# Multiplying the first three patches of an early-fusion block side by side, one piece of weights at a time

## The reference, cut to what matters

```python
xc = jnp.concatenate([x] + [_shift2d(x, HALF * s[2], HALF * s[0]) for s in shifts], axis=1)
patches = ...                      # [32, 36, 3840]
xn = (patches - mu) * jax.lax.rsqrt(var + LN_EPS) * ln_gamma + ln_beta
h = jnp.einsum('bnp,dp->bnd', xn, W) + b
h = jnp.concatenate([h, txt], axis=1)          # 36 patches and 128 text tokens
h = h + attention(layernorm(h))                # a decaying linear memory, 8 heads
h = h + experts(layernorm(h))                  # 2 of 8 gated experts per token
```

## Time and profile before

| | us |
|---|---|
| median of 3 runs | 548.85 (548.56 to 549.72) |
| span of the profiled execution | 547.2 |
| median less span | 1.65 |
| PE busy | 484.7 (89%) |
| DVE busy | 375.3 (69%) |
| ACT busy | 304.8 (56%) |
| mean granted TensorE clock | 0.962 |

### The profile page before, as it was taken

One profiled execution on the slowest core, in us unless ns is written; L12 is line 12 of the kernel. 1 busy time (PEld: TensorE's weight loads), 2 busy tenths in 40 slices (PEclk: granted clock), 3 DMA queues, 4 the chain that ended last, 5 costly groups with the idle time before them and its releaser, 6 DMA issues.

```text
span 547.2 us, 12568 instructions
## 1 busy us (share of the span) xinstructions
PE 484.7 (89%) x3157; PEld 461.4 (84%) x3158; DVE 375.3 (69%) x1293; ACT 304.8 (56%) x773; POOL 192.3 (35%) x272
## 2 busy tenths in 40 slices
PE   2999998998798987789999999999999999999900
PEld 2999997887576876789999999999999999999800
DVE  4969996459789879848566566565565565565597
ACT  5485967449578876435444444444444444444473
POOL 1000000006577777733333333333433433433330
PEclk9999999999799989799999999999999999999965
DMA  8988214711433342542222222222222222235897
GB/s 322 415 331 350 63 53 130 283 38 51 120 94 110 101 126 76 139 117 73 71 76 76 68 79 73 68 82 70 68 83 69 69 83 68 68 84 145 273 353 223
DMA packets 62463, 71.67 MB, mean 131 GB/s; under 512 B 19057, under 2 KB 56626, under 8 KB 61410
## 3 DMA queue, kind: packets, MB, share of 16 engines
q1 hardware_dynamic: 49920, 51.43, 30.6%
q0 software_dynamic: 8208, 16.95, 8.7%
q10 hardware_dynamic: 4306, 2.95, 1.8%
HBM read 49.43 MB, written 21.86 MB: 130 GB/s over the span
## 4 chain that ended last, share of the span: by engine, by line
PE 71%; DVE 15%; DMA 6%; ACT 4%; issue 2%; ACTq 1%; SPq 0%; POOL 0%; DVEq 0%; POOLq 0%
PE bank L838 8%; PE pair L838 6%; PE bank L1088 5%; PE bank L1084 5%; PE bank L1087 5%; PE bank L1086 5%; PE bank L1085 5%; PE bank L1095 5%; PE pair L1104 4%; PE bank L1104 4%; PE pair L1073 3%; PE pair L983 3%; ACT yall L749 2%; PE pair L987 2%; PE pair L1106 2%
## 5 line engine op out<-in xcount | busy, mean ns | idle before, releaser
L782 POOL DMA_INDIRECT disp<-xf,posu x82 | 85.0, 1037 | 151.0 <-ACT xf L654 123.8
L1575 DVE TENSOR_TENSOR hh<-sg,bank 128x384 f32<-128x384 f32 x89 | 49.3, 554 | 99.5 <-ACT sg L730 99.5
L812 POOL DMA_INDIRECT ydram<-ysb,dnow x89 | 88.5, 994 | 69.4 <-DMA ydram<-ysb,dnow 35.1
L730 ACT ACTIVATE sg<-bank 128x384 f32<-128x384 f32 x89 | 43.7, 492 | 116.8 <-PE bank L1088 116.8
L1084 PE MATMUL bank<-wa,xh 128*128 x178 | 67.5, 379 | 0.0
L1088 PE MATMUL bank<-wa,xl 128*128 x178 | 60.4, 339 | 0.0
L1087 PE MATMUL bank<-wa,xh 128*128 x178 | 59.9, 337 | 0.0
L1085 PE MATMUL bank<-wa,xh 128*128 x178 | 59.7, 336 | 0.0
L1086 PE MATMUL bank<-wa,xl 128*128 x178 | 59.7, 335 | 0.0
L809 POOL COPY dnow<-dest 128x1 uint32 (+1 forms) x89 | 16.9, 190 | 114.2 <-DVE ysb L1585 104.8
L838 PE MATMUL bank<-wcT,imgT 128*128 128x193 f32 x240 | 41.7, 335 | 10.6 <-DMA imgT<-in_pixels 10.6
(11 more groups left out here) (262 smaller groups left out, 1171.2 us busy)
## 6 DMA issues: line engine op xcount, KB each, us to landing
xs<-disp SPq DMA_DIRECT2D x89, 96.0 KB, 2.0
band<-in_bands SPq DMA_DIRECT2D x4, 1536.0 KB, 12.1
yall<-ydram SPq DMA_DIRECT2D x7, 768.0 KB, 7.8
imgT<-in_pixels SPq DMA_DIRECT2D x4, 768.0 KB, 12.5
imgT<-in_pixels SPq DMA_DIRECT2D x2, 1536.0 KB, 16.0
hres<-in_text SPq DMA_DIRECT2D x1, 3072.0 KB, 25.5
wa<-in_gate_up_w SPq DMA_DIRECT2D x8, 384.0 KB, 8.5
ring<-in_gate_up_w SPq DMA_DIRECT2D x32, 96.0 KB
```

Of the source, the lines that this page charges most:

```text
L782: pool.indirect_dma_start(disp, bass.IndirectOffsetOnAxis(ap=posu[c % XBUF][:, 2 * j + k:2 * j + k + 1], axis=0), xfd[c % XBUF][:, j, :], None
L812: pool.indirect_dma_start(ydram, bass.IndirectOffsetOnAxis(ap=dnow[b][:], axis=0), ysb[r][:], None).then_inc(s_ys[b], 16)
```

## The change

Pixels and weights come in pairs: behind piece g of the weights, row block g of the pixels with all four column blocks. PE multiplies patches 0, 1 and 2 by piece g before it goes on to piece g+1, each patch in its own bank; the three groups of sums are open at the same time. The two bands follow all four pairs; before, they stood ahead of the last pixels that patch 2 reads.

```diff
-            weights_in(0)
-            weights_in(1)
-            pixels_in(0, slice(0, 2), slice(0, 2))
-            weights_in(2)
-            pixels_in(1, slice(2, 4), slice(0, 2))
-            weights_in(3)
-            pixels_in(2, slice(0, 4), 2)
+            for g in range(4):
+                weights_in(g)
+                pixels_in(g, slice(g, g + 1), slice(0, 4))
             for i in range(2):
                 sp.dma_start(band[i][:], bands[:, i]).then_inc(s_band[i], 16)
-            pixels_in(3, slice(0, 4), 3)
             pixels_in(4, slice(4, 6), slice(0, 4))
...
             def patch(p):
-                i, j = p // 3, p % 3
-                if p:
-                    pe.wait_ge(s_img[1 + j if i == 0 else 3 + i], 16)
+                if p % 3 == 0:
+                    pe.wait_ge(s_img[3 + p // 3], 16)
                 if p >= 4:
                     pe.wait_ge(s_patout, p - 3)
...
-            for p in range(3):
-                patch(p)
+            for dr in range(4):
+                pe.wait_ge(s_wprep, dr + 1)
+                pe.wait_ge(s_img[dr], 16)
+                for p in range(3):
+                    ins = pixel_row(p, dr)
+                    if dr == 3:
+                        ins.then_inc(s_pat, 1)
```

More of the change, by code:

```diff
@@ L826, in patch, with pixel_row @@
             def patch(p):
-                i, j = p // 3, p % 3
-                if p:
-                    pe.wait_ge(s_img[1 + j if i == 0 else 3 + i], 16)
+                if p % 3 == 0:
+                    pe.wait_ge(s_img[3 + p // 3], 16)
                 if p >= 4:
                     pe.wait_ge(s_patout, p - 3)
[L832 to L837, removed]
+                for dr in range(4):
+                    ins = pixel_row(p, dr)
+                ins.then_inc(s_pat, 1)
+            def pixel_row(p, dr):
+                i, j = p // 3, p % 3
+                for k in range(6 * dr, 6 * dr + 6):
+                    s, c = k // 3 % 2, k % 3
                     ins = pe.matmul(bank[PATCH_BANK[p % 4]][:, 0:193], imgT[:, 2 * i + dr, j + s, c, :], wcT[:, k, :],
                                     start=(k == 0), stop=(k == 23))
-                ins.then_inc(s_pat, 1)
-            for p in range(3):
-                patch(p)
+                return ins
+            for dr in range(4):
+                pe.wait_ge(s_wprep, dr + 1)
+                pe.wait_ge(s_img[dr], 16)
+                for p in range(3):
+                    ins = pixel_row(p, dr)
+                    if dr == 3:
+                        ins.then_inc(s_pat, 1)
             pe.wait_ge(s_red, 2)
```

## The result

| | before | changed |
|---|---|---|
| median, us | 549.29 (4 runs) | 546.28 (4 runs) |
| ratio, 95% interval | | 0.9947 [0.9924, 0.9969] |
| ratio in two later sets of 12 runs | | 0.9951 [0.993, 0.9972] and 0.9958 [0.9941, 0.9976] |
| span of the profiled execution, us | 547.2 | 546.3, later 544.6 and 545.0 |

The change makes the kernel faster by 0.5%, 3.0 us by the first medians and 2.5 and 2.3 by the later ones; 2.4 and a time of 546.4 were forecast. Of most kernels a few executions are several microseconds longer than the rest (556.51 us among the twelve of the first later set); the ratios leave them out. In the first profile of the changed kernel the span shrinks by 0.9 us only: the execution that was profiled took 548.08 us, the slowest of its four.

What follows compares the result with a forecast made beforehand. PE alone was taken to bound the kernel's head through patch 8. Its start 2.42 us earlier, passed in full, gave a span of 547.2 - 2.4 = 544.8, plus 1.65 to the median: 546.4 us, range 545.5 to 547.8.

Steps and rivals of the forecast that it cites:

- The start: First transfers: row block 0 lands at 8.07, PE starts at 8.20 instead of 10.62, 2.42 us earlier (bounds 2.1 to 3.3).
- The slow head: PE's first records: slow spacing after idleness, paid once wherever the first matmul stands, so moving the start doesn't save it.
- 13 slow records and 2.03 us: Head of PE before: first 13 records take 4.16 us, 0.320 each instead of 0.164, costing 2.03 us.
- the slow head grows: Rival at PE's head: 8 more slow records cut the gain to 1.2 us, 13 more to 0.4; chance 0.11.
- late operands: Alternative cause of patch 0's 2.03 us: the new order would remove them too, gain 4.4 us rather than 2.42.
- Order of the matmuls at no price: First three patches on PE: three open sums cost nothing, later rows of 18 matmuls take 5.90 us, PE doesn't stall.
- The cover at piece 1: PE's second row: piece 1 ready at 14.1, wanted at 16.1, the nearest cover, 2.0 us.
- Behind the three patches: DVE's first read-out starts 1.8 us earlier, at 35.4; covers at the router and patch 8 let PE's gain pass in full.
- a worst case: DVE at patch 8: if it gains nothing, 0.6 us of its 3.04 us wait remain; if 1.8, 2.4 remain.
- Row block 0 came by itself: Answers a rival: row block 0 lands only with piece 1 at 10.49, gain 0 to 0.9 us; chance 0.09.
- The router's row: Rival before patch 3: PE waits at L850 for the router, gain gone if DVE is 5.3 us later; chance 0.04.
- To the end unchanged: Behind patch 8: no work is tied to absolute time, so the 2.42 us carry to the end.

Runs made afterwards that it cites:

- text_split: Changed kernel with the text in two transfers, the eight tiles DVE wants first apart and ahead: 546.57 us against 548.59 before, ratio 0.9972.
- pixels_behind_second: Changed kernel with the first row block of pixels put behind the second piece of weights: 550.17 us against 550.07 before, ratio 0.9999.
- matmuls_alone: Kernel before with only the new order of matmuls, transfers in the old order: 561.96 us against 550.07 before (one run).
- warm_head: Changed kernel with 12 idle matmuls on PE ahead of the wait for the first pixels: 546.29 us against 548.59 before, ratio 0.994.
- first_pixels_split: Changed kernel with row block 0 in two transfers, patch 0's two column blocks first: 546.44 us against 548.59 before, ratio 0.9957.

## Why the prediction was right

**The bound.** PE set the stage before and sets it after: moving its start moves the end (ratio 0.9951), putting the start back takes it away (0.9999), and relieving DVE alone brings nothing that can be told (text_split).

**The start.** Row block 0 landed at 8.39, and 8.11 to 8.66 over the three profiles of the changed kernel if one takes off the 0.14 us to the first matmul, against 8.07 forecast. The step held and its size was off: 2.09 us of gain at the first matmul (1.82 to 2.37) instead of 2.42. Of the two neighbours by which I bounded it, the upper (8.4) was the nearer.

**The slow head.** It is paid at the new start as well, as forecast, but its size is not one number. From the first matmul to `red` it took 25.49 us before (10.62 to 36.11 on the timeline) and 25.86, 25.41 and 26.61 in the changed kernel; without slow records 23.78. By that measure 1.71 us were paid before, and 1.6 to 2.8 after. The prediction's 13 slow records and 2.03 us were misread: the line of the earlier trace rows counts the records that start before 14.5 us, and its 4.16 us hold the run-out of the last one. By the single starts of that trace the second record follows 0.457 us behind the first, ten more follow at 0.321, and from 14.29 on they are 0.164 apart; together that is 1.87 us more than at 0.164 throughout, the figure to set against 2.03. The rival "the slow head grows" came true in one of the three profiles, where it took 1.1 us of the gain; in the others it took at most 0.4. But the head of before was a short one, as the seven profiles in the last section show, and the longest of all, 26.67 us, is that of pixels_behind_second, which starts at 10.03: no run ties a longer head to the earlier start. By the Trainium skill, page "TensorE: Matmul & The Clock Gate", section "What's actually happening", activity releases the slow state. The trace agrees: with idle products from 2.65 on, the first real matmul at 8.57 runs at the spacing of 2.4 GHz, 0.164 us. The window of matmuls_alone ties the spacing to the clock: after 3.46 us without work the records from 18.30 on are again 0.32 us apart, and the granted clock of the window 18.0 to 21.3 reads 0.50. That late operands made the slow head, and the gain would be 4.4 us, is excluded.

**Order of the matmuls at no price.** It held: three open sums run at 5.91 us a row of 18, as forecast (5.90), and no wait stands between rows. The cover at piece 1 was 16.68 (start of the second row on PE's timeline) less 14.07 (11.88 + 2.19), 2.6 us; at the router 35.12 (PE's L851) less 33.68 (33.37 + 0.31), 1.4 us. One term of that sum was slightly off: it let DVE start piece 3 when it lands, at 17.9, though by its own figures DVE is busy with piece 2 to 18.2; DVE started it at 18.24.

**Behind the three patches.** This is the step that failed: "DVE starts its first read-out at 35.4 instead of 37.22, 1.8 us earlier". It did (35.62, 1.60 earlier), but I took it that the gain lasts. The text transfer, which I had not placed in the queue, is what it meets. SP's timeline and the rows of DMA issues (KB each, us from issue to landing) show it, before:

```profile
13.81 0.44 SPq L426 DMA_DIRECT2D hres<-in_text  x1
hres<-in_text SPq DMA_DIRECT2D x1, 3072.0 KB, 25.5
```

and changed:

```profile
7.37 0.83 SPq L421 DMA_DIRECT2D hres<-in_text  x1
hres<-in_text SPq DMA_DIRECT2D x1, 3072.0 KB, 31.6
```

SP issued it at 13.81 before and issues it at 7.37 now, so it landed at 39.3 and lands at 39.0: the bytes ahead of it are the same. DVE had come for it at 39.30 before, just as it landed, and a wait of nothing hid how tight that was. DVE's wait for patch 8 was 1.72 us, where 2.4 was forecast. The prediction had priced a worst case (DVE gains nothing, 0.6 us remain), and with it the forecast stood. A PE gain much over 3 us would have been lost here: warm_head and first_pixels_split, with patch 8 read 2.97 and 2.87 us earlier than before, have 0.54 and 0.79 us of DVE's wait left.

**The rivals.** Row block 0 came by itself (8.39, piece 1 at 10.49). The router's row was 1.4 us ahead of PE, and is waited for only when the slow head is gone too (0.40 us in warm_head). Only the slow head took a share, in one profile.

**To the end unchanged.** Right in the mean, not in the single profile. Patch 8 is read 1.72, 2.45 and 0.71 us earlier, the first expert load 0.54, 2.26 and 2.66, the span 0.9, 2.6 and 2.2, and the medians 3.0, 2.5 and 2.3. The first scatter keeps patch 8's gain to 0.05 us in all three (123.90, 123.22 and 124.91 against 125.62). From it to the first load the kernel of before takes 105.32 us and the changed one 106.50, 105.46 and 103.37: a scatter of 3.1 us, to which the landing of one transfer (3.70 to 6.01 us) adds most; without it 1.5 us are left (99.67 to 101.16), in the gaps between the scatters of rows. What stays open: patch 8 gains 1.6 us and the span 1.9 in the mean, where the medians gain 2.3 to 3.0. Part of it may be the one profile of before, whose slow head was short: the six other profiles without idle products and without stalls average 26.09 us to `red`, and with such a head before, an estimate of the gain at patch 8 is 1.6 + 0.6 = 2.2 us. With one profile of before, this can't be settled.

That 546.28 lies within 0.2 us of the 546.4 forecast is partly luck. The gain was right in mechanism and near in size (2.42 forecast, 2.3 to 3.0 by the medians), but the same changed kernel measured 547.54 and 546.74 in the later sets, beside 550.07 and 549.04 for the kernel before.

## What to carry to other kernels

When the first product waits for the second of several large operands in one queue, ask how much of that operand the first pieces need, and reorder the products so that what has landed is used by all sums that want it; the transfers and the products must move together: here the new products alone lost 12 us, and the new transfers alone gained nothing. Place every transfer behind the moved ones in the queue, not only those that the bound engine reads. Then look at how much the other engines lag: here 1.7 us of lead for DVE were left, and further gains for PE alone fell into it.

## What the runs showed of the hardware

The slow head of TensorE varies from execution to execution with the same work: over seven profiles with no idle products 25.41 to 26.67 us from first matmul to `red`, 1.6 to 2.9 above the 23.78 without it. The granted clock of the windows reads 1.00 there all the same, and so it does in a window in which PE has done nothing yet:

```profile
5.00:10.00 5.00, 0.00 (x0) 0.00 (x0) 2.92 (x3) 3.77 (x11) 0.00 (x0) 1.00 1.00 363
```

The trace of before holds no record of the clock until 14.28 us, the very place where the spacing halves; in the three profiles of the changed kernel the first record stands at 12.96, 11.76 and 14.75 us, again where it halves. So a 1.00 ahead of that record says nothing, and the spacing has to be read.

An indirect scatter, issued every 1.26 us, lands in 2.6 us by the median, but the one that the first expert waits for took 3.70 to 6.01 us in these profiles, and moves the next stage by as much. Why, no run here shows.

SP needed 4.62 us to issue the two bands before and 1.11 in the changed kernel, where the queue's packets are 48896 instead of 49920. The text was issued 6.4 us earlier, with the same bytes ahead of it, and landed 0.3 us earlier: here the landing followed the bytes ahead in the queue and not the time of issue.
